# The second feed-forward layer as one float32 product in place of three float32r products

## What is computed

```python
xn = layernorm(x)                      # x: 2 batches x 1024 tokens x 128
out = x + attention(xn) + ffn(xn)
# ffn: router picks 3 of 8 zones for each batch, with weights w
pooled = xn.mean(axis=1)
probs  = softmax(tanh(pooled @ W1 + b1) @ W2 + b2)
top_p, top_i = top_k(probs, 3);  w = top_p / top_p.sum()
for e in picked zones:                 # Wa[e]: 128 x 512, Wb[e]: 512 x 128
    z = gelu(xn @ Wa[e]) @ Wb[e]
    zone_outputs += z * w[e]
ffn = xn + zone_outputs
# attention: 16 subheads of width 8 with rotary embedding, softmax over 1024 keys,
# the difference of two softmaxes for each of 8 heads, rms norm, output projection
```

## Time and profile before

| | before |
|---|---|
| median of 3 runs (lowest to highest) | 548.88 us (548.57 to 549.22) |
| the profiled execution, its own time | 547.23 us |
| its span in the trace, instructions | 545.4 us, 8613 |
| TensorE (PE) busy, matmuls | 517.8 us (95%), 2607 |
| TensorE weight loads (PEld) busy | 295.6 us (54%), 2607 |
| VectorE (DVE) busy | 458.2 us (84%), 800 |
| ScalarE (ACT) busy | 339.3 us (62%), 424 |
| GpSimd (POOL) busy | 68.8 us (13%), 69 |
| mean granted TensorE clock | 0.981 of full |

### The profile page before, as it was taken

The page is one execution under the profiler, slowest core; times in us unless marked ns, Lnnn a source line. Parts: engine busy times, 40 slices in busy tenths (PEclk is TensorE's granted clock), DMA queues, the critical chain, the costliest instruction groups (busy, mean ns, idle before and its releaser), DMA issues.

```text
span 545.4 us, 8613 instructions
## 1 busy us (share of the span) xinstructions
PE 517.8 (95%) x2607; PEld 295.6 (54%) x2607; DVE 458.2 (84%) x800; ACT 339.3 (62%) x424; POOL 68.8 (13%) x69
## 2 busy tenths in 40 slices
PE   6586999999999999999999999999999999999995
PEld 5564677777555554545555454555545455554333
DVE  2986778999889999999999999999999999998116
ACT  1440687666757666675766666666666666666872
POOL 3186961300000000000000000000000000000000
PEclk9697999999999999999999999999999999999999
DMA  9135526100000010020002001000200020000002
GB/s 314 53 108 199 176 100 199 55 1 2 0 2 1 13 58 2 1 70 0 1 1 67 1 0 46 23 1 0 69 1 0 2 67 3 0 2 1 2 2 77
DMA packets 11771, 23.46 MB, mean 43 GB/s; under 512 B 1490, under 2 KB 6226, under 8 KB 11618
## 3 DMA queue, kind: packets, MB, share of 16 engines
q1 hardware_dynamic: 11314, 20.34, 11.7%
q10 hardware_dynamic: 432, 2.81, 1.4%
HBM read 14.43 MB, written 8.39 MB: 42 GB/s over the span
## 4 chain that ended last, share of the span: by engine, by line
PE 74%; DVE 14%; DMA 4%; ACT 3%; issue 2%; POOL 1%; SPq 1%; ACTq 0%; DVEq 0%; POOLq 0%
PE ps L994 24%; PE ps L1023 23%; PE ps L1016 22%; DVE part_max L683 4%; DVE hL L722 4%; DMA X<-in_x 2%; ACT h L478 1%; PE ps L937 1%; DVE wbH L628 1%; DMA q_scr<-ropeL 1%; ACT hH L481 1%; DVE wbL L630 1%; DMA wb_raw<-in_wb 1%; PE ps L1010 1%; PE ps L862 1%
## 5 line engine op out<-in xcount | busy, mean ns | idle before, releaser
L683 DVE TENSOR_REDUCE part_max<-ps 128x1 f32<-128x512 f32 x512 | 340.1, 688 | 25.4 <-PE ps L994 22.3
L512 ACT ACTIVATE E<-ps 128x1024 f32<-128x1024 f32 x256 | 248.2, 1022 | 125.0 <-PE ps L1016 125.0
L994 PE MATMUL ps<-K,Q 128*128 128x512 f32 x512 | 193.7, 421 | 0.8 <-DVE part_max L683 0.3
L1016 PE MATMUL ps<-Q,K 128*128 128x512 f32 x512 | 161.4, 399 | 0.2 <-ACT zT L486 0.2
L994 PEld LDWEIGHTS ps<-K,Q 128*128 128x128 f32 x512 | 96.0, 188 | 119.3 <-DVE part_max L683 100.7
L1023 PE MATMUL ps<-E,Vg 128*32 128x512 f32 x1024 | 136.4, 605 | 0.6 <-ACT E L512 0.6
L1016 PEld LDWEIGHTS ps<-Q,K 128*128 128x128 f32 x512 | 94.8, 188 | 27.7 <-ACT E L512 10.3
L417 POOL TENSOR_TENSOR U<-AT,rsum 128x256 f32 (+1 forms) x15 | 9.3, 623 | 392.2 <-DVE rsum L776 392.2
L478 ACT ACTIVATE h<-ps 128x512 f32<-128x512 f32 x48 | 28.6, 595 | 38.0 <-PE ps L864 30.8
L722 DVE TENSOR_TENSOR hL<-h,hH 128x512 fp32r<-128x512 f32 x48 | 37.8, 802 | 8.0 <-ACT hH L481 8.0
L1023 PEld LDWEIGHTS ps<-E,Vg 128*32 128x32 f32 x1024 | 20.1, 108 | 44.7 <-issue 34.9
(11 more groups left out here) (140 smaller groups left out, 321.9 us busy)
## 6 DMA issues: line engine op xcount, KB each, us to landing
Q<-q_scr SPq DMA_DIRECT2D x8, 512.0 KB
K<-k_scr SPq DMA_DIRECT2D x32, 96.0 KB
tab<-in_tables ACTq DMA_DIRECT2D x1, 2048.0 KB, 11.4
q_scr<-ropeL SPq DMA_DIRECT2D x4, 512.0 KB, 5.7
q_scr<-ropeH SPq DMA_DIRECT2D x4, 512.0 KB, 4.6
k_scr<-ropeH SPq DMA_DIRECT2D x4, 512.0 KB, 5.1
wa_raw<-in_wa SPq DMA_DIRECT2D x6, 256.0 KB, 3.0
wb_raw<-in_wb SPq DMA_DIRECT2D x6, 256.0 KB, 3.6
```

Of the source, the lines that this page charges most:

```text
L512: nc.scalar.activation(E[:, par, 2 * jj:2 * jj + 2, :].rearrange("p j t -> p (j t)"), ps[:, 2 * jj:2 * jj + 2, :].rearrange("p j t -> p (j ...
L683: nc.vector.tensor_reduce(part_max[:, half, col, sh:sh + 1], ps[:, ring_bank(x), :], AX.X, ALU.max).then_inc(slot_read, 1)
L994: mm(ps[:, ring_bank(x + sh), :], Q[:, g % 2, k // GJ * P:(k // GJ + 1) * P], K[:, g % 2, k % GJ, sh * BANK:(sh + 1) * BANK], start=True, ...
L1016: last = mm(ps[:, j, :], K[:, par, j, st * P:(st + 1) * P], Q[:, par, th * BANK:(th + 1) * BANK], start=True, stop=True)
```

## The change

`second` becomes one product of the float32 `wb_f` with the float32 `h`. The copy to hH (ScalarE), the subtraction to hL (VectorE) and the subtraction to wbL (VectorE) are gone, with their semaphores. `wb_zone` keeps its multiplication, which now writes `wb_f`. Gelu writes straight into a ring of four float32 buffers and waits for `hs_free` itself. `second` waits for `gelu_done`. The first layer, the loads, GpSimd's program and all of attention are the same. Both programs compute the whole reference.

```diff
@@ -175,12 +175,10 @@
-        (wa_raw, wb_raw, waH, waL, wbH, wbL, h, hH, hL, rot), r4 = region(
+        (wa_raw, wb_raw, waH, waL, wb_f, h, rot), r4 = region(
             r3, ("wa_raw", [P, 2, FF], F32), ("wb_raw", [P, 2, FF], F32),
             ("waH", [P, 2, FF], F32R), ("waL", [P, 2, FF], F32R),
-            ("wbH", [P, 2, FF], F32R), ("wbL", [P, 2, FF], F32R),
-            ("h", [P, 2, BANK], F32),
-            ("hH", [P, H_BUFS, BANK], F32R), ("hL", [P, H_BUFS, BANK], F32R),
+            ("wb_f", [P, 2, FF], F32), ("h", [P, H_BUFS, BANK], F32),
             ("rot", [P, ROT_BUFS, 2, BANK], F32))
...
@@ -475,10 +472,8 @@
             def gelu(n, s):
                 act.wait_ge(g1_done, n + 1)
-                nc.scalar.activation(h[:, s % 2, :], ps[:, 6 + s % 2, :], ACT.Gelu_apprx_tanh).then_inc(gelu_done, 1)
-                act.wait_ge(gelu_done, n + 1)
                 act.wait_ge(hs_free, n + 1)
-                nc.scalar.activation(hH[:, s % H_BUFS, :], h[:, s % 2, :], ACT.Copy).then_inc(hh_done, 1)
+                nc.scalar.activation(h[:, s % H_BUFS, :], ps[:, 6 + s % 2, :], ACT.Gelu_apprx_tanh).then_inc(gelu_done, 1)
@@ -492,7 +487,6 @@
                 for s in range(2 * UZ):
                     if not (last and s + 2 >= 2 * UZ):
-                        act.wait_ge(split_done, 2 * UZ * it + s + 1)
                         gelu(2 * UZ * it + s + 2, s + 2)
@@ -625,10 +619,7 @@
-                nc.vector.tensor_scalar(wbH[:, par, :], wb_raw[:, par, :], w, None, ALU.mult).then_inc(wbh_done, 1)
-                dve.wait_ge(wbh_done, e + 1)
-                nc.vector.scalar_tensor_tensor(wbL[:, par, :], wb_raw[:, par, :], w, wbH[:, par, :],
-                                               ALU.mult, ALU.subtract).then_inc(wb_split, 1)
+                nc.vector.tensor_scalar(wb_f[:, par, :], wb_raw[:, par, :], w, None, ALU.mult).then_inc(wb_done, 1)
@@ -715,12 +706,8 @@
-            def split_turn(it, lead, last):
+            def ffn_turn(it, lead, last):
                 for s in range(2 * UZ):
-                    n = 2 * UZ * it + s
-                    dve.wait_ge(hh_done, n + 1)
-                    nc.vector.tensor_tensor(hL[:, s % H_BUFS, :], h[:, s % 2, :], hH[:, s % H_BUFS, :],
-                                            ALU.subtract).then_inc(split_done, 1)
                     if s == FC:
                         wb_zone(2 * it + 1)
@@ -933,10 +920,8 @@
             def second(s, par, end):
                 c, f, buf = CB * par + s % UZ // FC, s % FC, s % H_BUFS
                 fs = slice(f * P, (f + 1) * P)
-                for i, (l, r) in enumerate(((wbH, hH), (wbH, hL), (wbL, hH))):
-                    last = mm(ps[:, c, :], l[:, par, fs], r[:, buf, :], start=False,
-                              stop=end and f == FC - 1 and i == 2, skip_group_check=True)
-                last.then_inc(hs_free, 1)
+                mm(ps[:, c, :], wb_f[:, par, fs], h[:, buf, :], start=False, stop=end and f == FC - 1,
+                   skip_group_check=True).then_inc(hs_free, 1)
@@ -957,8 +942,8 @@
                     if s % UZ == 0:
-                        pe.wait_ge(wb_split, 2 * it + s // UZ + 1)
-                    pe.wait_ge(split_done, n + 1)
+                        pe.wait_ge(wb_done, 2 * it + s // UZ + 1)
+                    pe.wait_ge(gelu_done, n + 1)
                     second(s, s // UZ, last and s >= UZ)
```

More of the change, by code:

```diff
@@ L226, in build @@
         dch = sem("dch")
[L228 to L231, removed]
+        wah_done, wa_split, wb_done = sem("wah_done"), sem("wa_split"), sem("wb_done")
+        g1_done, gelu_done, hs_free, z_out, zt_done, res_done = (
+            sem("g1_done"), sem("gelu_done"), sem("hs_free"), sem("z_out"), sem("zt_done"), sem("res_done"))
         slot_made, slot_read, neg_done, maxh_done = (
@@ L263, in raw_next @@
                 sp.sem_inc(sp_waited, 1)
-                sp.wait_ge(wb_split, e + 1)
+                sp.wait_ge(wb_done, e + 1)
                 raw_load(e + 2)
@@ L732, in split_turn @@
                         residual(sum_chunk(s, 6))
-            split_turn(0, False, False)
+            ffn_turn(0, False, False)
             dve.wait_ge(lam_exp, 1)
@@ L755, in _ @@
                                            ALU.mult, ALU.add).then_inc(comb_done, 1)
-            split_turn(TOP_K - 2, True, False)
-            split_turn(TOP_K - 1, True, True)
+            ffn_turn(TOP_K - 2, True, False)
+            ffn_turn(TOP_K - 1, True, True)
             for u in range(4 * UZ - 2, 4 * UZ):
```

## The result

| | before | after |
|---|---|---|
| median, 8 runs each (lowest to highest) | 549.05 us (548.43 to 550.25) | 551.86 us (550.29 to 552.78) |
| the profiled execution, its own time | 547.23 us | 551.17 us |
| its span, instructions | 545.4 us, 8613 | 549.4 us, 8369 |
| mean granted TensorE clock | 0.981 | 0.981 |

The ratio is 1.0046, with a 95% interval of 1.0031 to 1.006: the changed kernel is slower by 2.8 us by the medians and by 2.5 us by the ratio (1.7 to 3.3 by the interval). That is more than the 0.2% taken as the bound of no change. It lies in the range of the prediction, but the likeliest case there was no change.

What follows compares the result with a forecast made beforehand. TensorE, busy 96% or more in all three stretches, was taken as the bound. An earlier start (-0.9) and a longer score-product stretch (+1.2) gave +0.3 us: 549.2 us from the median of 548.88, range 547.3 to 554.

Steps and rivals of the forecast that it cites:

- Price of a unit: Second layer on TensorE: one float32 product 0.86 us against 0.70 for three float32r, +0.16 us in each of 48 units.
- rival 1: Second layer: each change of product type exposes weight loads; 552.9 us at 0.1 a unit, 564.4 at 0.34; chance 0.22.
- Start of the feed-forward: Without the wbL subtraction TensorE resumes at 51.4, second(0) starts at 55.9 and not 59.23, score products reached at 87.9.
- What holds that place next: First score product: the load of Q becomes the bound, its chain 0.9 us shorter, start at 89.0 in place of 89.9.
- The stretch with score products: Units 20 to 47: more product time, fewer waits for VectorE; 53.7 us in place of 52.5, +1.2 us.
- rival 2: Score-product stretch: waits come from the exchange of two banks and stay; 551.2 to 552.4 us; chance 0.20, shared with sizes off.

Runs made afterwards that it cites:

- b_kfill: The kernel before with GpSimd's fills of K and `maxones` put ahead of waH and waL of zone 2; 547.52 us, ratio 0.9965.
- before_again: The kernel before, unchanged, in another execution for its trace; 548.78 us (span 547.0).
- after_again: The changed kernel, unchanged, in another execution for its trace; 552.67 us (span 550.9).
- a_warm: The changed kernel with ten products whose results nothing reads put ahead of the wait for K and Q; 550.29 us, ratio 1.0019.
- a_kfill: The changed kernel with GpSimd's fills of K and `maxones` put ahead of waH and waL of zone 2; 547.36 us, ratio 0.9968.
- a_kfill_dve: `a_kfill` with one unread VectorE subtraction of hL's size added in each unit; 555.36 us, ratio 1.0133.
- hyb_kfill: The kernel before with the float32 product in units 0 to 15 only and GpSimd's fills moved ahead; 544.44 us, ratio 0.9916.
- hyb: `hyb_kfill` with GpSimd's fills back in their old place; 550.48 us, ratio 1.003.
- b_rot: The kernel before with zone 0's wbL subtraction moved behind the last rotary products; 549.57 us, ratio 1.0011.

## Why the prediction was right and wrong

**Price of a unit: right.** Predicted 1.40 + 0.16 = 1.56 us. TensorE's timeline of the changed kernel:

```profile
69.88 1.02 PE L923 MATMUL ps<-h,wb_f 128*128 128x512 f32 x2
70.33 0.79 PE L849 MATMUL ps<-xnH,waH 128*128 128x512 f32 x1
70.96 0.40 PE L850 MATMUL ps<-xnL,waH 128*128 128x512 f32 x1
71.20 0.39 PE L851 MATMUL ps<-xnH,waL 128*128 128x512 f32 x1
71.43 1.02 PE L923 MATMUL ps<-h,wb_f 128*128 128x512 f32 x2
```

71.43 - 69.88 = 1.55, in two records a call, 96 in all. The next product starts in step, so nothing is lost where the types meet, and rival 1 is out. The Trainium skill (TensorE: Matmul & The Clock Gate, section on weight-path perf modes) excludes FP32 weights from its fast weight load. These traces show no loss by it: the float32 weight loads of L923 take 191 ns, those of L850 192:

```profile
L923 PEld LDWEIGHTS ps<-h,wb_f 128*128 128x128 f32 x96 | 18.3, 191 | 4.3
...
L850 PEld LDWEIGHTS ps<-xnL,waH 128*128 128x128 f32 x48 | 9.2, 192 | 6.5 <-issue 5.5
```

**Start of the feed-forward: right.** Predicted: TensorE resumes at 51.4, `second(0)` at 55.9, the clock holds, score products reached at 87.9. Measured 51.31, 55.83, full clock from 53.83 to 57.24, and 88.0. The clock was in part luck: the reason given was 2.0 us idle and not 3.5, but waits of 2.49 (`b_kfill`) and 2.66 us (`before_again`) at this place ended once in the half clock and once not. The wait was 1.56 here, and the clock held in every trace with 1.2 to 1.7 us there.

**What holds that place next: right in kind, wrong in size, and this is the step that failed.** The prediction named the load of Q as the new bound and had it release the score products at 89.0, 0.9 us sooner than before. They started at 90.80 and 91.69, against 89.89 and 91.56 before: no gain. GpSimd's part did shrink. GpSimd and SP of the changed kernel:

```profile
60.34 1.28 POOL L372 TENSOR_TENSOR rope<-rot 128x512 f32<-128x512 f32 x1
...
67.03 0.61 POOL L362 CAST waH<-wa_raw 128x512 fp32r<-128x512 f32 x1 [3.38 <-PE ps L851]
...
68.94 7.21 POOL L390 MEMSET K<- 128x8192 f32 x1
```

```profile
56.40 1.18 SPq L281 DMA_DIRECT2D q_scr<-ropeH  x2
57.62 1.50 SPq L281 DMA_DIRECT2D q_scr<-ropeL  x1
63.62 0.34 SPq L254 DMA_DIRECT2D wa_raw<-in_wa  x1
```

`rope` takes 1.28 us (1.71 to 1.76 in the two traces of the kernel before beside VectorE's subtractions) and waH 0.61 (before 1.01). By the Trainium skill (SBUF, section on who interferes with whom) a VectorE instruction with two SBUF inputs contends with a GpSimd instruction that reads SBUF. These numbers agree. But little of the time won arrives. The places of the chain in the four traces of the two kernels (us):

| | before | `before_again` | changed | `after_again` |
|---|---|---|---|---|
| GpSimd ends ropeL of m = 5 | 55.4 | 56.1 | 55.2 | 54.9 |
| SP issues the writes to q_scr | 55.53 | 56.72 | 56.40 | 56.12 |
| SP issues zone 2's raw load | 62.79 | 63.96 | 63.62 | 63.34 |
| GpSimd starts waH of zone 2 | 66.22 | 67.40 | 67.03 | 66.87 |
| GpSimd starts the fill of K | 68.86 | 69.84 | 68.94 | 68.77 |
| SP issues the load of Q | 85.16 | 86.14 | 85.55 | 85.34 |
| first score product | 89.9 | 91.6 | 90.8 | 91.7 |

The faster rope gains nothing: in the changed kernel the writes to q_scr go out 1.2 us after GpSimd is ready, because SP first waits for the earlier writes to k_scr to land (`scr_out`). Only in the first trace of the kernel before, on which the prediction was built, did they go out as soon as GpSimd was ready. From there to waH each step is a DMA landing. SP waits 4.2 us for q_scr before it issues the raw load, and GpSimd waits 3.38 us for that load, which lands 3.4 us after its issue; the first-layer product that the row names had long been done. The faster waH and waL do arrive, 0.5 to 0.7 us between the fourth row and the fifth. Then the last step takes them back: from the issue of the load of Q to the first score product are 4.7 and 5.4 us before, and 5.3 and 6.4 in the changed kernel. Why the load lands later there no run tells. The prediction had seen that wait, said that it absorbs most, and then took 0.9 all the same. And it measured from an execution where the load was early: its base had the score products at 89.89, where `before_again` has 91.56, of which 1.0 us had gone before the load was issued.

**The clock behind the wait: missed.** The prediction priced the wait of about 1 us as idle time alone. It was 2.8 and 3.9, and the clock fell to half behind it: 1.6 us more, which `a_warm` gives back. The half clock behind a wait at the start had been costed, but not for the wait that the change creates. No rival had it either. The range (547.3 to 554) took the result in by its room for rivals 1 and 2, neither of which happened; that it holds is luck.

**The stretch with score products: right.** Predicted 53.7 us; 53.8 in `a_warm` and 53.6 in `a_kfill`, where the clock does not fall. The waits go with hL, as said: the wait for row maxima before the transpose of `neg_max` was 0.65 (predicted 0.6), and rival 2 is out. (Its lower price, +2.3, left out the 0.9 from the start that its upper one, +3.5, had taken off.) That VectorE's load made those waits is not shown (`a_kfill_dve`). `before_again` took 52.3 us (91.56 to 143.90) and `b_kfill` 52.2, so the stretch is +1.4 to +1.5 where +1.2 stood.

The sum, against a usual execution of the kernel before:

| term | predicted | measured |
|---|---|---|
| release of the first score product | -0.9 | 0 |
| stretch with score products, full clock | +1.2 | +1.4 |
| half clock behind the wait | 0 | +1.6 |
| sum | +0.3 | +3.0 (medians: +2.8; ratio: +2.5) |

The first row is the least certain. Against `before_again` the score products start 0.8 us sooner in one trace of the changed kernel and 0.1 later in the other; against the first trace of the kernel before they start 0.9 and 1.8 later. Pair by pair (first with first, again with again) the spans differ by 4.0 and 3.9 us, with 0.2 and 0.8 of it in attention and the tail. That is more than the medians say, so the sum closes to about 1 us and not better.

The direction of the error is the lesson: the 2 to 3 us that the change wins at the start vanished in the wait, and the wait then cost 1.6 us more through the clock.

## What to carry to other kernels

Where an edit brings TensorE sooner to a place that a load bounds, cost the wait at more than its length: here 2.8 us of it were followed by 1.6 us lost to the clock, and moving two fills ahead on GpSimd was worth 4.3 us in the changed kernel, against 2.7 for the best choice of products with the load out of the way (`hyb_kfill` against `b_kfill`; both by the ratios). One float32 product in place of three float32r ones costs TensorE 0.16 us and takes 0.75 us off VectorE and 0.6 off ScalarE (36.0 and 29.1 us over 48 units). In this kernel it paid to use it in the units where the splits hold TensorE up, and the split form where their time is covered: 0.84% with the fills moved, of which the move alone is 0.35%. And look at the bound in more than one execution before a change of 1 us is costed against it: the landing of this load moved by 1.7 us between two traces of the same kernel.

## What the runs showed of the hardware that was not expected

- TensorE's granted clock fell to half behind waits for the load of 2.8 and 3.9 us (changed kernel) and 5.1 (`hyb`), behind 3.5 and 2.49 at the start (kernel before, `b_kfill`) and at the end of a wait of 2.1 for hL (`b_rot`). It did not behind 0.54 (`before_again`), 0.76 (`b_rot`) and 0.42 (`a_warm`) before the score products, nor behind the 1.2 to 1.7 us at the start of the kernels with the float32 product, nor behind 2.66 us at the start of `before_again`. Waits of 2.1 and 2.49 us were followed by the half clock and one of 2.66 was not, so the length of a wait alone did not decide. In the changed kernel the clock was back after 3.4 us.
- VectorE stood still for 2.8 us twice in the attention loop when 48 small instructions had been added ahead of it, 5.6 us in all, with 21 instruction packets on q14 in place of 11, three of them around each stall. A control that adds instructions to an engine can cost more by such stalls than by the work it was meant to add.
- The scaling of one zone's Wb on VectorE, took 0.48 us at 53.59 in the changed kernel, started just ahead of a GpSimd subtraction that then took 1.52 in place of 1.28. Elsewhere beside GpSimd's work it took 0.92 and 1.40, and 3.05 in `a_kfill_dve`. Smaller work can lose more: a scaling of 128x64 (L740), 0.26 us in `after_again`, took 5.10 in the changed kernel and ended at 76.20, as GpSimd's fill of K did (68.94 to 76.15). It held nothing up here:

```profile
71.10 5.10 DVE L740 TENSOR_SCALAR comb<-cst,lt 128x64 f32<-128x64 f32 x1
```

```profile
70.92 3.05 DVE L623 TENSOR_SCALAR wb_f<-wb_raw,wbc 128x512 f32<-128x512 f32 x1
```
